# A fused attention and gated-FFN layer in FP32: projection split at column 384, v staged by VectorE, and a reciprocal root without its separate semaphore increments

## What is computed

```python
xn = layernorm(x)
# attention: 32 query heads in 8 groups of 4, one k and one v head per group, head size 128
q, k, v = xn @ Wq.T, xn @ Wk.T, xn @ Wv.T
q, k = rmsnorm(q, q_norm_w), rmsnorm(k, k_norm_w)      # v is not normalised
scores = einsum('bkgqd,bksd->bkgqs', q, k) / sqrt(128)
attn = softmax(scores + alibi_bias_and_causal_mask)
s = einsum('bkgqs,bksd->bkgqd', attn, v) @ Wo.T
# gate
g = silu((silu(xn @ w_gate.T) * (xn @ w_up.T)) @ w_down.T)
out = x + s * g
```

## Time and profile before

| what | us |
|---|---|
| median of 3 runs | 2520.85 (2518.89 to 2521.02) |
| the profiled execution: device time | 2519.08 |
| the profiled execution: span, first to last instruction | 2517.3 |
| TensorE busy | 2443.9 (97% of the span) |
| VectorE busy | 1692.9 (67%) |
| ScalarE busy | 1233.5 (49%) |
| GpSimd busy | 782.9 (31%) |
| mean granted TensorE clock | 0.993 of full speed |

### The profile page before, as it was taken

One profiled execution on the slowest core, in us unless ns is written; L12 is line 12 of the kernel. 1 busy time (PEld: TensorE's weight loads), 2 busy tenths in 40 slices (PEclk: granted clock), 3 DMA queues, 4 the chain that ended last, 5 costly groups with the idle time before them and its releaser, 6 DMA issues. The chain is left out here.

```text
span 2517.3 us, 39632 instructions
## 1 busy us (share of the span) xinstructions
PE 2443.9 (97%) x13232; PEld 2070.5 (82%) x13232; DVE 1692.9 (67%) x3709; ACT 1233.5 (49%) x2548; POOL 782.9 (31%) x2154
## 2 busy tenths in 40 slices
PE   5999999999999999999989999999999999998998
PEld 4888888888888888788878888888888888887887
DVE  5777777786877777823257777777777777777132
ACT  3545555454545554543345455555554555545333
POOL 3313132322322323244433232323241313231443
PEclk8999999999999999999989999999999999999999
DMA  2000000000000000023320101000000000010223
GB/s 110 18 26 18 26 18 26 18 26 18 26 18 26 18 8 36 26 76 134 109 76 1 43 1 36 8 26 18 26 17 26 18 26 18 1 43 9 93 90 111
DMA packets 22858, 92.33 MB, mean 37 GB/s; under 512 B 6528, under 2 KB 6656, under 8 KB 18560
## 3 DMA queue, kind: packets, MB, share of 16 engines
q1 hardware_dynamic: 22656, 89.80, 10.3%
HBM read 85.60 MB, written 4.19 MB: 36 GB/s over the span
## 5 line engine op out<-in xcount | busy, mean ns | idle before, releaser
L511 ACT ACTIVATE pT_hi<-ring_ps 128x512 fp32r<-128x512 f32 x576 | 343.7, 599 | 547.3 <-PE ring_ps L336 536.2
L688 DVE TENSOR_TENSOR pT_lo<-ring_ps,pT_hi 128x512 fp32r<-128x512 f32 x576 | 394.4, 688 | 66.9 <-ACT pT_hi L511 63.3
L503 ACT ACTIVATE probs<-probs,low_min 128x896 f32<-128x896 f32 (+7 forms) x512 | 394.9, 773 | 53.9 <-DVE low_min L680 53.8
L680 DVE CUSTOM_DVE_ANT_0 probs<-score_ps,rel_sb,slope 128x512 f32<-128x512 f32 (+3 forms) x512 | 329.1, 645 | 27.6 <-PE score_ps L325 14.5
L336 PE MATMUL ring_ps<-ident,probs 128*128 128x128 f32 x2304 | 346.8, 274 | 0.7 <-DVE probs L698 0.7
L850 POOL TENSOR_SCALAR rs_x<-sq_sum 128x5 f32<-128x5 f32 x128 | 25.5, 199 | 1014.5 <-DVE sq_sum L647 945.2
L336 PEld LDWEIGHTS ring_ps<-ident,probs 128*128 128x128 f32 x2304 | 278.1, 140 | 51.0 <-issue 1.3
L325 PE MATMUL score_ps<-kv_hi,qT_hi 128*128 128x512 f32 (+3 forms) x768 | 283.1, 369 | 15.5 <-DVE natural L653 8.4
L349 PE MATMUL out_ps<-pT_hi,kv_hi 128*128 128x512 f32 x576 | 266.3, 462 | 3.1 <-DVE pT_lo L688 2.7
L325 PE MATMUL score_ps<-kv_hi,qT_lo 128*128 128x512 f32 (+3 forms) x768 | 268.0, 349 | 0.0
L325 PE MATMUL score_ps<-kv_lo,qT_hi 128*128 128x512 f32 (+3 forms) x768 | 266.1, 347 | 0.0
(11 more groups left out here) (135 smaller groups left out, 5306.2 us busy)
## 6 DMA issues: line engine op xcount, KB each, us to landing
qkv_raw<-w_ffn_dram SPq DMA_DIRECT2D x44, 768.0 KB, 4.2
qkv_raw<-w_qkv_dram SPq DMA_DIRECT2D x16, 1536.0 KB, 6.8
o_raw<-w_o_dram SPq DMA_DIRECT2D x16, 1024.0 KB, 4.8
probs<-x_dram SPq DMA_DIRECT2D x4, 1024.0 KB, 7.2
o_raw<-x_dram SPq DMA_DIRECT2D x4, 1024.0 KB, 6.8
out_dram<-y SPq DMA_DIRECT2D x16, 256.0 KB, 3.7
rel_sb<-rel_dram SPq DMA_DIRECT2D x1, 512.0 KB, 11.4
inv_slope<-inv_slopes_dram SPq DMA_DIRECT2D x16, 2.5 KB, 1.6
```

Of the source, the lines that this page charges most:

```text
L503: act.activation(row, row, ACT.Exp, scale=-1.0, bias=low_min[:, i % 2, h, HEAD_CHUNKS[i] - 1:HEAD_CHUNKS[i]], accum_out=row_sum[:, i % 2, ...
L511: act.activation(pT_hi[:, n % SLOTS, :], ring_ps[:, ring_bank(r), :], ACT.Copy).then_inc(ring_high, 1)
L680: dve.tensor_tensor_reduce(out=probs[i % 2][:, h, lo:hi], in0=score_ps[:, n % 2, 0:hi - lo], in1=rel_sb[:, at:at + hi - lo], scale=slope[: ...
L688: dve.tensor_tensor(out=pT_lo[:, n % SLOTS, :], in0=ring_ps[:, ring_bank(r), :], in1=pT_hi[:, n % SLOTS, :].bitcast(F32), op=ALU.subtract) ...
```

## The change

The change does five things together:

1. `project` splits the 768 columns as 384 + 384, each half at the start of its own PSUM bank (q heads 0 to 2 in one, q head 3, k and v in the other).
2. `square` covers all 768 columns, and `sum_squares` makes 6 sums instead of 5. The sixth is not used. `rq` gets a sixth column that is set to 1.0 once.
3. `scale_qk` writes 768 columns, v times 1.0 among them, into one of 3 buffers (`natural_of`). `stage_v`, `v_nat`, the semaphore `v_staged` and its waits are gone; `split_v` reads `natural` after `qk_done`. From the fourth tile on `scale_qk` waits for `v_split` of three tiles earlier.
4. `rsqrt` makes the product with `inv_slope` on the side (into `rs_z`, after the seventh instruction), and the last instruction writes `rq` directly. The number of instructions of `norms` stays 13; the dependent ones are 12. `x_norms` keeps its 12, and `normalise_x` waits for a semaphore of its own.
5. The separate increments of `pool_passed` (in `chained`, `split`, `norms`, `x_norms`) and `dve_passed` (in `bias`, `row_stats`) are gone.

```diff
-CHAIN = 12
+CHAIN = 11
...
-        natural = sb("natural", [P, 3 * NQK])
-        qk = [natural[:, k * NQK:(k + 1) * NQK] for k in range(2)]
-        qk_sq = natural[:, 2 * NQK:3 * NQK]
-        v_nat = sb("v_nat", [P, VBUFS, P])
+        natural, qkv_sq = sb("natural", [P, NBUFS, NW]), sb("qkv_sq", [P, NW])
...
+        def natural_of(t):
+            return natural[:, (t - 1) % NBUFS, :]
+        def two_banks(acc):
+            return acc.rearrange("p (a n) -> p a n", a=2)[:, :, 0:HALF]
...
                     pe.wait_ge(qk_done, tile(U, i) - 1)
-                    pe.wait_ge(v_staged, tile(U, i) - 1)
...
-                        pe.matmul(acc[:, 0:BANK], a, w[:, c, 0:D], start=go, stop=end)
-                        mm = pe.matmul(acc[:, BANK:BANK + KV], a, w[:, c, D:NW], start=go, stop=end)
+                        pe.matmul(acc[:, 0:HALF], a, w[:, c, 0:HALF], start=go, stop=end)
+                        mm = pe.matmul(acc[:, BANK:BANK + HALF], a, w[:, c, HALF:NW], start=go, stop=end)
...
-                act.activation(qk_sq, acc[:, 0:(G + 1) * P], ACT.Square).then_inc(squared, 1)
-
-            def stage_v(acc, i, t, early):
-                if not early:
-                    act.wait_ge(v_split, t - VBUFS)
-                act.activation(v_nat[:, i % VBUFS, :], acc[:, BANK + P:BANK + KV], ACT.Copy).then_inc(v_staged, 1)
+                act.activation(qkv_sq[:, :].rearrange("p (a n) -> p a n", a=2), two_banks(acc), ACT.Square).then_inc(squared, 1)
...
-            def scale_qk(acc, i, t):
+            def scale_qk(acc, t):
                 dve.wait_ge(rq_done, t)
-                dve.wait_ge(v_staged, t)
...
+                if t > NBUFS:
+                    dve.wait_ge(v_split, t - NBUFS)
+                dve.tensor_tensor(out=natural_of(t).rearrange("p (a g n) -> p a g n", a=2, n=P),
+                                  in0=two_banks(acc).rearrange("p a (g n) -> p a g n", n=P),
+                                  in1=rq[:, :].rearrange("p (a g) -> p a g", a=2).unsqueeze(3).to_broadcast([P, 2, GROUPS // 2, P]),
+                                  op=ALU.mult).then_inc(qk_done, 1)
...
                 dve.wait_ge(scored, U * SCORES + n + 1)
-                dve.sem_inc(dve_passed, 1)
...
                 ins.then_inc(pool_chain, 1)
                 pool.wait_ge(pool_chain, done + count)
-                pool.sem_inc(pool_passed, 1)
...
                 chained(pool.tensor_tensor(out=aa, in0=yy, in1=yy, op=ALU.mult), done, 7)
+                if factor is not None:
+                    pool.tensor_tensor(out=zz, in0=yy, in1=factor, op=ALU.mult).then_inc(pool_side, 1)
                 chained(pool.tensor_tensor(out=aa, in0=aa, in1=xx, op=ALU.mult), done, 8)
...
-                chained(pool.tensor_tensor(out=yy, in0=aa, in1=yy, op=ALU.mult), done, 12)
+                if factor is not None:
+                    pool.wait_ge(pool_side, out_done)
+                    pool.tensor_tensor(out=out, in0=aa, in1=zz, op=ALU.mult).then_inc(rq_done, 1)
+                else:
+                    pool.tensor_tensor(out=out, in0=aa, in1=yy, op=ALU.mult).then_inc(x_rs_done, 1)
...
-                    pool.tensor_tensor(out=rq[:, :], in0=rs_y[:, TILES:TILES + G + 1], in1=inv_slope[:, :], op=ALU.mult).then_inc(rq_done, 1)
...
-                    pool.wait_ge(v_staged, tile(U, i))
+                    pool.wait_ge(qk_done, tile(U, i))
```

More of the change, by code:

```diff
@@ L33 @@
 NQK = (G + 1) * P
-VBUFS = 4
+NBUFS = 3
+HALF = NW // 2
+GROUPS = NW // P
 GATES = 3
@@ L399, in step @@
                         turn_q(U, (i + 1) % TILES, RING_AT[i] + BEFORE[i], first, tile(U, i + 1))
-                        turn_k(U, (i + 1) % TILES, RING_AT[i] + BEFORE[i] + 1, first)
+                        turn_k(U, (i + 1) % TILES, RING_AT[i] + BEFORE[i] + 1, first, tile(U, i + 1))
                     if 0 <= k - LAG < turns:
@@ L723, in normalise_x @@
             def normalise_x(row, half):
-                dve.wait_ge(pool_chain, (row * CHAINS + half + 1) * CHAIN)
+                dve.wait_ge(x_rs_done, row * HALVES + half + 1)
                 for t in range(half * HT, (half + 1) * HT):
@@ L754, in step @@
                             bias(U, 0, k)
-                        scale_qk(qkv_ps, 1, tile(U, 1))
+                        scale_qk(qkv_ps, tile(U, 1))
                         low_q(U, 1, RING_AT[0] + BEFORE[0])
@@ L758, in step @@
                         sum_squares(tile(U, 2), False)
-                        scale_qk(first_ps, 0, tile(U, 2))
+                        scale_qk(first_ps, tile(U, 2))
                         sum_squares(tile(U, 3), False)
@@ L789, in step @@
                         if k == 2 and not (last and i >= TILES - 2):
-                            scale_qk(qkv_ps, (i + 2) % TILES, tile(U, i + 2))
+                            scale_qk(qkv_ps, tile(U, i + 2))
                         if ahead and turns and k == turns + 1:
@@ L800, in unit @@
                             low_x(b, t)
-                        scale_qk(first_ps, 0, tile(U, 0))
+                        scale_qk(first_ps, tile(U, 0))
                         sum_squares(tile(U, 1), False)
@@ L886, in x_norms @@
                 pool.wait_ge(mv_done, row * TILES + (half + 1) * HT)
-                pool.sem_inc(pool_passed, 1)
-                rsqrt(mv[:, at, 1], at, 1.0, LN_EPS, (row * CHAINS + half) * CHAIN)
+                rsqrt(mv[:, at, 1], at, 1.0, LN_EPS, None, rs_y[:, at], row * HALVES + half + 1, (row * CHAINS + half) * CHAIN)
             for half in range(HALVES):
@@ L917, in split_v @@
                         pool.wait_ge(weighed, U * TURNS)
-                    pool.wait_ge(v_staged, tile(U, i))
-                    split(v_hi[:, i * P:(i + 1) * P], v_lo[:, i * P:(i + 1) * P], v_nat[:, i % VBUFS, :], v_high, tile(U, i), v_split)
+                    pool.wait_ge(qk_done, tile(U, i))
+                    split(v_hi[:, i * P:(i + 1) * P], v_lo[:, i * P:(i + 1) * P], natural_of(tile(U, i))[:, NQK:NW], v_high, tile(U, i), v_split)
                 def step(U, i, first, last):
```

43 lines of the change are left out of this document (17 added, 26 removed).

## The result

| | us | ratio to before, 95% interval |
|---|---|---|
| before | 2519.92 (2518.89 to 2521.02, 4 runs) | |
| changed | 2490.49 (2488.17 to 2491.73, 4 runs) | 0.9882 [0.9865, 0.9899] |
| forecast | 2506.5 (2495 to 2517) | |

What follows compares the result with a forecast made beforehand. TensorE, busy 97% of the span, was taken as the bound, its gaps mattering. From 2519.1 us, 11.6 (step 1) and 7.2 (first units) less and 4.6 (halves) more gave 2504.9, 2506.7 on the median's scale; predicted 2506.5, range 2495 to 2517.

Steps and rivals of the forecast that it cites:

- The chain of step 1: Square, sums, GpSimd's root and scaling, in sequence, delay the projection in step 1; real gap 1.30 us per unit.
- 80 ns of idle time in a link: GpSimd's root: idle time per dependent link falls from 192 to 80 ns without the increment.
- `rq` 3.41 us after the first of the thirteen: GpSimd's root, start of first instruction to complete `rq`: 3.41 us instead of 4.80, taken as 1.4 less.
- the sum of 0.37: Tile chain: wider square, sums and scaling add 0.11 + 0.13 + 0.13 = 0.37 us.
- a gap 0.83 shorter: Step 1 of units 2 to 8, both rows: gap falls from 1.30 to 0.47 us, 14 times, 11.6 us less.
- Rival A: GpSimd's increments are free, so the longer chain and dearer matmuls make the kernel slower, 2529 us; chance 0.08.
- The term of the halves: Projection in 384 + 384 columns: 3 ns more per pair, 4.6 us more; bounds 3 less to 12 more.
- 1.0 less: Individual exposed chains in the rows' first units: each gap 1.0 us shorter, from 1.4 - 0.37.
- rival C: More is won by faster `bias`, free halves and fuller clock in the first units: 2497 us; chance 0.17.
- the term of 0.8 for the first weights: Kernel start: GpSimd reaches the weight chunks sooner, so the gap at 24.98 goes, 0.8 us less.
- I count zero, between 6 less and 3 more: VectorE elsewhere: less work per tile and no increments before 768 `bias` give zero; bounds 6 us less, 3 more.
- Behind it I expect nothing to take its place: After the step 1 gap of units 2 to 8: no new wait appears behind the shortened gap; no further change.

Runs made afterwards that it cites:

- b_v: Changed kernel with all but v's staging by VectorE and the wider instructions undone (512 + 256 columns, increments, serial root back): 2535.15 us, ratio 1.0059.
- a_early: Changed kernel with the scaling of step 1 put ahead of the `bias` of slot 2 on VectorE: 2486.44 us, ratio 0.9868.
- b_nopool: Kernel before, with only GpSimd's separate semaphore increments taken out: 2491.05 us, ratio 0.9888.
- a_512: Changed kernel with the projection in 512 + 256 columns again, v still staged by VectorE: 2493.50 us, ratio 0.9898.
- b_warm: Kernel before, with unread 512-column matmuls filling three gaps of each row's first unit: 2516.18 us, ratio 0.9984.
- a_warm: Changed kernel with unread matmuls in three gaps of each row's first unit and before two late output projections per row: 2484.72 us, ratio 0.9861.
- a_dveinc: Changed kernel with VectorE's separate increments put back: 2492.25 us, ratio 0.9890.
- b_nodve: Kernel before, with only VectorE's separate increments (before `bias` and in `row_stats`) taken out: 2513.79 us, ratio 0.9976.

## Why the prediction was wrong

**Right.** The chain of step 1 as what the change acts on; 80 ns of idle time in a link without the increment (83); `rq` 3.41 us after the first of the thirteen (3.44); the widths of the wider instructions and the sum of 0.37 (b_v: 0.37); a gap 0.83 shorter (0.84), with VectorE's `bias` late next (a_early). Rival A fell with b_nopool.

**The term of the halves had the wrong sign.** The step "I take 3 ns per pair: 4.6 us more" failed. The two rows I had, 353 and 354 ns, said no change; the 3 ns rested on an impression that projection matmuls start a little later than score matmuls of the same width, which is true of 512 columns, and so was already in the 353 of the pair to be replaced. Measured: 350 ns, 3.0 us less (a_512). The term was off by 7.6 us, half of the 14.2 us by which the profiled execution beat the sum.

**The first units were priced by their gaps alone.** The steps "1.0 less" and their like were near: 6.7 shown for 5.8. What failed is that nothing was priced for the clock behind a gap, although showed two slices at 8 tenths, and the working left that to rival C at 0.17. That this clock costs time is shown: filling the gaps of before gives 4.0 us with nothing else changed (b_warm), filling those of the changed kernel another 5.8 (a_warm). What the change itself won by it is only bounded. The two first units together came out 5.1 us beyond the forecast, of which 1.0 is the halves and 0.9 the gaps named above. The lower-clock stretches in them fell by 10.2 us, worth at most 5.1. Another 1.0 to 1.2 is the faster start of the profiled execution, which is luck: the term of 0.8 for the first weights was near where the starts are alike (1.0 in a_early). How the remaining 2 us or so divide between the gaps and the clock isn't separated.

**VectorE's increments were priced at zero.** "I count zero, between 6 less and 3 more": measured 6 less alone, 1.8 in the changed kernel. The value lay in the bounds, but the row for it was at hand: an increment behind a wait had just been priced at 110 ns on GpSimd, and the same line stands ahead of 768 `bias`.

By place, the profiled execution beat the sum by 9.4 us in the steady units, of which 6.6 are the halves, by 5.1 in the first units, and lost 0.3 elsewhere. VectorE's increments hold 0.6 to 1.4 of the steady units (0.04 each in a_dveinc, 0.10 in b_nodve). Another 1.1 went against the step "Behind it I expect nothing to take its place": it looked only for what would be late next, and the shorter chain also ended the late weightings, 0.08 us in each steady unit. Some 0.05 in each is assigned by no run.

**What the parts are worth.** GpSimd's increments: 28.7 us alone, 23.4 as the last to go. The halves: 3.0. VectorE's increments: 1.8 to 6. The side product of the root: 1.1 with the increments gone, within the spread, and some 15 by subtraction with the increments and the wider instructions in place. The staging by VectorE costs 15 us in the kernel before, where the chain is exposed. As the last part it cost 2491.05 - 3.0 - 1.8 - 1.1 = 2485.2 against 2490.49, so some 5 us; that is by subtraction and assumes that the parts add up. The kernel that keeps the other parts with v copied by ScalarE was not run.

## What to carry to other kernels

Price every bookkeeping instruction that stands between a wait and the work behind it, on the engine where it stands: find the nearest row with the same wait and without it, and take the difference times its count along the exposed chain. Then look at the clock row ahead of and behind each gap: a gap costs its own length and the slower stretch that may follow, and filler matmuls tell the two apart. Before an instruction on a chain is widened, look at which chains are hidden by less than it adds; and for two shapes that differ by less than the rounding of the rows, take zero and keep both signs.

## What the runs showed of the hardware

- A bare semaphore increment between a wait and an instruction of 5 elements per partition cost about 110 ns on GpSimd (192 to 83 ns idle in the link, b_nopool). Without it a link of dependent small instructions is 0.28 us.
- One access over two PSUM banks costs nothing that shows: 768 columns as 2 x 384 took 816 ns on ScalarE and 951 on VectorE in the mean, on the slope of the rows at 512 and 640.
- A pair of 384 + 384 columns is 3 ns shorter than one of 512 + 256 (350 and 353), 3.0 us over the kernel.
- After gaps of 1.65 to 4.06 us TensorE ran at its lower level for 3.4 to 10.2 us in the first units (before and changed). Matmuls that nothing reads, placed in the gaps, took most of it away: 23.8 us in the changed kernel fell to 3.4 (a_warm), for 5.8 us of time.
